# Gates' products at unit 4 in passes one and two, and one decay formed ahead of their Silu

## The chip, the cores and the metric

The kernel runs on one core of a Trainium2 chip. Its time is the device time of one execution in microseconds (us), and lower is better. The engines that matter here are PE (TensorE, matmuls), DVE (VectorE), ACT (ScalarE), POOL (GpSimd) and SP (the queue that issues the DMAs). Each works through its own instructions in order and waits for the others at semaphores.

## The reference, cut to what matters

Thirty-two images of 257 tokens with 256 features go through a small tower: a tokenizer, a layer of four state-space (Mamba) blocks with a mixture of experts, and a layer of attention with a routed feed-forward part. The change lies in the state-space blocks alone:

```python
def _mamba_block(x, in_w, conv_w, conv_b, A_log, xd_w, xB_w, xC_w, dtp_w, dtp_b, D, out_w, g, b):
    res = x
    xn = _layer_norm(x, g, b)
    xz = xn @ in_w
    xs, z = jnp.split(xz, 2, axis=-1)
    xc = conv(xs)                              # depthwise, 4 taps
    xc = silu(xc + conv_b)
    delta = softplus(xc @ xd_w @ dtp_w + dtp_b)
    Bm = xc @ xB_w
    Cm = xc @ xC_w
    A = -jnp.exp(A_log)
    dA = jnp.exp(delta[..., None] * A)         # the decays
    dBx = (delta * xc)[..., None] * Bm[:, :, None, :]
    y = _ssm_scan(dA, dBx, Cm) + D * xc        # h = dA_t * h + dBx_t ; y = sum_n h * C_t
    return y * jax.nn.silu(z) @ out_w + res    # silu(z): the gates
```

A block has 512 channels with 16 states each; two blocks run forward over the tokens and two backward.

## The kernel before

The program has two phases, the state-space blocks (`mamba_phase`) and the rest (`tail_phase`). The first takes the images in 16 groups of two. Each group has four jobs, one for each block. The first group's job 0 is written out ahead; a loop over 15 groups then holds jobs 1, 2, 3 and 4, where job 4 is job 0 of the next group; jobs 1, 2 and 3 of the last group follow. There are 64 jobs in all. "Pass one" and "pass two" are jobs 1 and 2.

A job is a scan over 64 states, 16 for each of four chunks of 128 channels. It is written as 32 units `u` of two states, `2u` and `2u+1`. For each state `s`:
- ACT forms the decay (L781), an Exp of 512 columns, into one of two banks (`decay`, by `s % 2`). It may do so once the scan of state `s-2` is through. ACT's unit `u` forms the decays `2u+2` and `2u+3`.
- POOL multiplies B by the input (`bu`, L543, four buffers).
- DVE scans (L982; L986 in the first chunk) and multiplies the result by C (L1002). For every fourth state POOL does this product (L555). The scans of a unit come first, its products behind them.
- PE adds the result to `y_ps` by transposes (L1239), in unit `u` the states `2u-2` and `2u-1`. With the first state of a chunk it multiplies the skip connection in front (L1232), which has to wait until ACT has copied the last chunk's rows out of `y_ps` to `y_t` (`token_rows`, L756; at units 1, 9, 17 and 25).

Everything else is placed by hand beside these units. The places the change touches are these:
- The gates of the job are four products `z0` to `z3` of PE (L1123, w_ps<-xn,in_w), one for each of the units from `gates_at(jj)`. ACT copies each to `sz` one unit later (L740). When all are there it takes the Silu of all of `sz` (L746). A table load stands in front of it, and one behind it (L747) brings the table for Exp and Ln back.
- The next job's norm begins at unit 9: PE forms the centred input in two products, `cen0` at unit 9 and `cen1` at unit 10 (L1123, w_ps<-x_f,mean_w and tok_mean, or x_b). ACT squares and copies each (L645, L648): the first behind decay 23, the second between decays 24 and 25.
- At unit 2 PE starts the last job's output projection, `o0` and `o1`, which ACT copies at units 4 and 5 (L767). DVE multiplies a chunk's rows by the gates (L1022), the first one in unit 13.

All products other than `y_ps` share three banks, `w_ps`. A table of names gives each product a slot; even slots use banks 0 and 1, odd ones 2 and 1, so each shares the middle bank with its neighbour. A bank is free when the readers of the earlier slot have counted up `work_read` for their parity. A name with one bank uses bank 0 or 2 alone.

```python
            def gates_at(jj):
                return 7 if jj == 4 else 5
            def silu_at(jj):
                return gates_at(jj) + 4, CONV_AT + 9
```

Of the kernel before, what the change touches and what calls it, by code (L numbers as in the profile page):

```python
# [5 lines left out]
ALU = mybir.AluOpType  # L6
# [19 lines left out]
DVE_C = STATES - len(POOL_C)  # L26
BLOCK_OF_JOB = (0, 2, 1, 3)
CONV_AT = 14
EPS = 1e-5
LOG_EXP = "natural_log_exp_and_others"  # L30
LN_SLACK = 2.0 ** -23
# [4 lines left out]
def mamba_phase(nc, a, h_mid, bc_dram, diag_dram, skip_dram):  # L36
# [18 lines left out]
    def one_job(jj, more):  # L55

        keys = [("y3", jj - 1)]
        keys += [("o0", jj - 1), ("o1", jj - 1)]
        keys += [("tmean", 4)] if jj == 3 and more else []
        keys += [("m0", 3), ("m1", 3)] if jj == 4 else []  # L60
        gates = [(name, jj) for name in gates_of_job]
        if jj == 3 and more:
            gates = gates[:1] + [("tvar", 4)] + gates[1:]
        return keys + gates + later_keys(jj, preparation(jj + 1, jj == 2 and more) if more or jj < 3 else [])
# [18 lines left out]

    def bank_count(name):

        return 1 if name in ("first", "y0", "y1", "y2", "y3") else NB

    slots = {key: i for i, key in enumerate(first_keys + body_keys)}
    final_slots = {key: n_first + i for i, key in enumerate(final_keys)}
# [6 lines left out]


    def gates_at(jj):
        return 7 if jj == 4 else 5

    def y_at(jj):
        return (14 if jj == 4 else 12), 18, 26
# [1 line left out]
    def silu_at(jj):  # L104

        return gates_at(jj) + 4, CONV_AT + 9

# [8 lines left out]
    def job_count(g, jj, per_job, k):  # L116

        return g * (4 * per_job) + (jj * per_job + k)
# [13 lines left out]
    def positive(count):  # L132

        return not isinstance(count, int) or count > 0
# [15 lines left out]
    with ExitStack() as ctx:  # L150
# [464 lines left out]
        def _(act):  # L615
# [150 lines left out]
                dst = o_f if jj % 4 == 2 else stream(jj)  # L766
                func(dst[:, c, :, :], w[:, :, 0:S], ACT.Identity).then_inc(read_of(name, g, jj), 1)  # L767

            def decays(g, jj, s):

                jj, s = on(jj, s)
                c, n = s // NST, s % NST
                k = BLOCK_OF_JOB[jj % 4]
                if n == 0 and c == 0:
                    act.wait_ge(delta_ready, job_count(g, jj, CI, c + 1))
                elif n == 0:
                    act.wait_ge(delta_reset, job_count(g, jj, CI - 1, c))

                if positive(job_count(g, jj, STATES, s + 1 - NDP)):
                    act.wait_ge(scan_done, job_count(g, jj, STATES, s + 1 - NDP))  # L780
                func(decay[:, s % NDP, :].rearrange("p (b t) -> p b t", b=NB), delta[:, c, :, 1:S], ACT.Exp,  # L781
                     scale=neg_a[:, k, c, n:n + 1]).then_inc(decays_ready, 1)

# [91 lines left out]
            def after_odd(g, jj, u, first, last):  # L875

                if u == 0:
                    softplus_powers(g, jj, 3)
                if u == 1:
                    softplus_log(g, jj, 3)  # L880
                if jj == 3 and not last and u == 5:
                    square_tokens(g, 4)
                if jj == 0 and u == 6 or jj == 4 and u == 8:
                    start_backward(g, jj + 1)
                if jj == 4 and u == 22:
                    copy_h(g, 4)
                if u == silu_at(jj)[0]:
                    gate_silu(g, jj)
                if last:
                    return  # L890
                if u == norm_at(jj) + 1:
                    centred(g, jj + 1, 0)
                if jj != 4 and u == norm_at(jj) + 4:
                    gain_and_bias(g, jj + 1)
                if u == CONV_AT + 1:
                    conv_input(g, jj + 1, 1)
                if u == silu_at(jj)[1]:
                    conv_silu(g, jj + 1)
                if u == CONV_AT + 11:
                    projections(g, jj + 1)  # L900
                if u in (CONV_AT + 12, CONV_AT + 13):
                    softplus_start(g, jj + 1, u - CONV_AT - 12)
                if u == CONV_AT + 14:
                    softplus_log(g, jj + 1, 0)
                if u == 31:
                    softplus_powers(g, jj + 1, 2)

            def lead(g, jj, s, last):

                if not (last and s >= STATES):  # L910
                    decays(g, jj, s)

            def period(g, jj, first, last):
                for u in range(UNITS):
# [15 lines left out]
        def _(dve):  # L930
# [34 lines left out]
            def h_slot(s):  # L965
                return len([v for v in range(s) if v not in POOL_C]) % NU

            def scan(g, jj, s, b):
                inside = s not in POOL_C
                if b == 0:  # L970
# [8 lines left out]
                h = h_ps[:, h_slot(s), :] if inside else ch[:, s % NPR, :]  # L979
                if s >= NST:  # L980

                    dve.tensor_tensor_scan(h, decay[:, s % NDP, :], bu[:, s % NBU, 0:NB * L], 0.0, ALU.mult, ALU.add  # L982
                                           ).then_inc(scan_done, 1)
                    return
                cols = slice(b * L, (b + 1) * L)
# [64 lines left out]
            def period(g, jj, first, last):  # L1050
                for u in range(UNITS):
# [15 lines left out]
                    if size:  # L1067
                        step_size(*size, 0)
                    scan(g, jj, s + 1, 0)
                    if s + 1 in POOL_C and s < NST:  # L1070
                        c_times_h(g, jj, s)
                        scan(g, jj, s + 1, 1)
                    else:
                        if s < NST:
                            scan(g, jj, s + 1, 1)
                        c_times_h(g, jj, s)
                        if s + 1 not in POOL_C:
                            c_times_h(g, jj, s + 1)
# [949 lines left out]
```

## Time and profile before

| | us |
|---|---|
| median of 3 runs | 10204.22 (10203.43 to 10209.12) |
| the profiled execution | 10211.62 |
| its span, first to last instruction | 10209.9 |
| mean granted clock of PE, as a share of the full one | 0.886 |

Over the span DVE is busy 79%, PE 81%, POOL 69% and ACT 58%. These shares mix two phases: in the state-space phase DVE and POOL are busiest, in the rest PE. The state-space phase ends near 8500 us. The clock stands in the profile as the share granted: 1.0 is 2.4 GHz and 0.5 is 1.2 GHz.

One logical matmul in float32 is two instructions in the trace, so a gate's product is a row of eight, and so is a pair of states. A timeline row gives its start, the time it covers, and in brackets how long the engine was idle before it and what ended that.

### The profile page before, as it was taken

Reading aid. Unit: us, or ns where it says so; the run is one execution under the profiler, and the core shown is the slowest. Engines: PE = TensorE matmul, PEld = TensorE weight load, DVE = VectorE, ACT = ScalarE, POOL = GpSimd, SP = SyncE. Lnnn points to the kernel's source line nnn. Section 1 sums busy time; section 2 is a strip of 40 time slices with the busy share of each in tenths; the row PEclk is TensorE's granted clock in tenths of the full one; section 3 lists DMA queues with packets and bytes.
Section 4 is the critical chain, followed back from the end, with each engine's and each line's share of the span. In section 5 each row is a group of like instructions: output and inputs, shape, how many; then the busy total and the mean of one; then the engine's idle time right before and its main releaser. Section 6 shows DMA issues by size and latency. Waiting matters only on the chain. (4 is left out here: it accounts for less than half of the span.)

```text
span 10209.9 us, 153036 instructions
## 1 busy us (share of the span) xinstructions
PE 8288.9 (81%) x42776; PEld 6783.2 (66%) x42776; DVE 8054.5 (79%) x10482; ACT 5907.1 (58%) x9202; POOL 7026.4 (69%) x7227
## 2 busy tenths in 40 slices
PE   5787878787878787878787878787878776999998
PEld 4666666666666666666666666666666664777776
DVE  4989898989898989898989898989898993333332
ACT  4656566666665666666666666666666662544443
POOL 4878788888888888888888888888888882000000
PEclk8888888888988888889898888888988887999998
DMA  2222222222222222222222222222222220000000
GB/s 92 99 90 94 100 94 98 95 99 94 97 97 91 94 96 96 98 96 94 89 89 86 94 94 100 94 99 93 100 94 100 94 84 24 11 12 8 12 10 9
DMA packets 414834, 818.78 MB, mean 80 GB/s; under 512 B 148918, under 2 KB 194138, under 8 KB 414042
## 3 DMA queue, kind: packets, MB, share of 16 engines
q1 hardware_dynamic: 410328, 806.69, 23.3%
q8 instruction: 331, 5.42, 0.2%
q14 instruction: 461, 3.78, 0.1%
q10 hardware_dynamic: 3714, 2.89, 0.1%
HBM read 783.16 MB, written 26.30 MB: 79 GB/s over the span
## 5 line engine op out<-in xcount | busy, mean ns | idle before, releaser
L781 ACT ACTIVATE decay<-delta,neg_a 128x512 f32<-128x512 f32 x4096 | 2799.4, 689 | 2378.0 <-DVE h_ps L982 1145.6
L543 POOL TENSOR_TENSOR bu<-b_all,u_buf 128x512 f32<-128x512 f32 x3072 | 3573.3, 1189 | 188.8 <-DVE h_ps L982 186.2
L982 DVE TENSOR_TENSOR_SCAN h_ps<-decay,bu 128x512 f32<-128x512 f32 x2304 | 2778.6, 1222 | 513.3 <-ACT decay L781 431.7
L1239 PE MATMUL y_ps<-ident,ch 128*128 128x128 f32 x16384 | 2504.0, 302 | 535.6 <-DVE ch L1002 412.8
L1239 PEld LDWEIGHTS y_ps<-ident,ch 128*128 128x128 f32 x16384 | 2132.8, 156 | 904.7 <-DVE ch L1002 552.4
L555 POOL TENSOR_TENSOR ch<-ch,c_all 128x512 f32<-128x512 f32 x1024 | 1326.3, 1295 | 966.9 <-DVE ch L982 779.1
L1002 DVE TENSOR_TENSOR ch<-h_ps,c_all 128x512 f32<-128x512 f32 x3072 | 1976.9, 671 | 0.0
L546 POOL TENSOR_TENSOR bu<-b_all,u_buf 128x514 f32<-128x514 f32 x1024 | 1244.8, 1236 | 12.7 <-DVE h_ps L982 9.1
L1123 PE MATMUL w_ps<-xn,in_w 128*128 128x257 f32 x4096 | 1095.1, 412 | 167.9 <-ACT xn L670 67.5
L986 DVE TENSOR_TENSOR_SCAN h_ps<-decay,bu 128x256 f32<-128x256 f32 x1536 | 1047.1, 737 | 59.2 <-POOL bu L546 33.9
L1123 PEld LDWEIGHTS w_ps<-xn,in_w 128*128 128x128 f32 x4096 | 806.9, 208 | 335.3 <-issue 75.7
L1582 POOL TENSOR_TENSOR rstd_F<-h_F 128x514 f32<-128x514 f32 x16 | 17.5, 1095 | 1425.6 <-DMA h_F<-h_mid 1425.6
L1123 PE MATMUL w_ps<-xs_pad,diag_store 128*128 128x257 f32 x4096 | 967.7, 381 | 10.5 <-ACT xc L697 10.5
L982 DVE TENSOR_TENSOR_SCAN ch<-decay,bu 128x512 f32<-128x512 f32 x768 | 923.5, 1202 | 23.7 <-ACT decay L781 22.3
L1123 PEld LDWEIGHTS w_ps<-xs_pad,diag_store 128*128 128x128 f32 x4096 | 741.7, 190 | 123.5 <-ACT xc L697 35.9
L1123 PE MATMUL w_ps<-sz,out_w 128*128 128x257 f32 x2048 | 498.9, 386 | 116.4 <-ACT x_b L767 52.4
L1123 PEld LDWEIGHTS w_ps<-sz,out_w 128*128 128x128 f32 x2048 | 375.4, 191 | 178.9 <-ACT x_b L767 59.7
L1123 PE MATMUL w_ps<-dtbc,dt_w 32*128 32x257 f32 x1024 | 397.5, 509 | 111.0 <-ACT rstd L723 107.4
L1232 PE MATMUL y_ps<-skip_diag,xc 128*128 128x128 f32 x2048 | 347.8, 324 | 150.1 <-ACT y_t L756 150.1
L1232 PEld LDWEIGHTS y_ps<-skip_diag,xc 128*128 128x128 f32 x2048 | 311.5, 230 | 213.7 <-ACT y_t L756 203.2
L1251 PE MATMUL w_ps<-ident,y_t 128*128 128x128 f32 x1024 | 187.0, 314 | 300.8 <-ACT y_t L756 300.8
L1123 PE MATMUL w_ps<-xc,xp_w 128*64 128x257 f32 x1024 | 270.9, 424 | 137.6 <-ACT xc L703 137.6
(262 smaller groups left out, 11512.5 us busy)
## 6 DMA issues: line engine op xcount, KB each, us to landing
b_all<-bc_dram SPq DMA_DIRECT2D x512, 514.0 KB, 6.4
c_all<-bc_dram SPq DMA_DIRECT2D x512, 514.0 KB, 7.4
in_w<-in_L_attn_in_w SPq DMA_DIRECT2D x64, 1024.0 KB, 5.0
diag_store<-diag_dram SPq DMA_DIRECT2D x256, 256.0 KB, 3.7
x_in<-in_x SPq DMA_DIRECT2D x128, 256.0 KB, 3.6
out_w<-in_L_attn_out_w SPq DMA_DIRECT2D x64, 512.0 KB, 3.9
skip_diag<-skip_dram SPq DMA_DIRECT2D x64, 256.0 KB, 4.4
h_mid<-h_cur SPq DMA_DIRECT2D x32, 257.0 KB, 2.2
```

The source lines that it names most:

```text
L543: pool.tensor_tensor(bu[:, s % NBU, 0:NB * L].rearrange("p (b t) -> p b t", b=NB), b_all[:, n // NU, n % NU, :, 1:], u_buf[:, c % 2, :, 1: ...
L546: pool.tensor_tensor(bu[:, s % NBU, :], b_all[:, n // NU, n % NU, :, :].rearrange("p b s -> p (b s)"), u_buf[:, c % 2, :, :].rearrange("p ...
L555: pool.tensor_tensor(h, h, c_all[:, n // NU, n % NU, :, 1:], ALU.mult).then_inc(pool_c_done, 1)
L781: func(decay[:, s % NDP, :].rearrange("p (b t) -> p b t", b=NB), delta[:, c, :, 1:S], ACT.Exp, scale=neg_a[:, k, c, n:n + 1]).then_inc(dec ...
L982: dve.tensor_tensor_scan(h, decay[:, s % NDP, :], bu[:, s % NBU, 0:NB * L], 0.0, ALU.mult, ALU.add).then_inc(scan_done, 1)
L986: last = dve.tensor_tensor_scan(h[:, cols], decay[:, s % NDP, cols], bu[:, s % NBU, b * S + 1:(b + 1) * S], bu[:, s % NBU, b * S:b * S + 1 ...
L1002: dve.tensor_tensor(ch[:, s % NPR, :].rearrange("p (b t) -> p b t", b=NB), h_ps[:, h_slot(s), :].rearrange("p (b t) -> p b t", b=NB), c_al ...
L1123: last = pe.matmul(w[0:rows, b, 0:S], lhs, rhs, start=(i == 0), stop=(i == len(terms(b)) - 1))
L1232: pe.matmul(y_ps[:, k, :], xc[:, jj % 2, c, b, 1 + half * P:1 + (half + 1) * P], skip_diag[:, jj % 2, c, :], start=(k == 0), stop=False, s ...
L1239: last = pe.matmul(y_ps[:, k, :], ch[:, s % NPR, k * P:(k + 1) * P], ident[:, :], is_transpose=True, start=False, stop=(n == NST - 1 and k ...
L1251: last = pe.matmul(w[:, k * P:(k + 1) * P], y_t[:, k, :], ident[:, :], is_transpose=True, start=True, stop=True, skip_group_check=True)
L1582: pool.tensor_tensor(rstd[s][:, :, :], h[s][:, 0, :, :], h[s][:, 1, :, :], ALU.add).then_inc(h_summed[s], 1)
```

## The change

- In every job but 3 and 4, `gates_at` is 4 instead of 5. Job 4 keeps 7 and job 3 keeps 5. The Silu, four units later, comes at unit 8 instead of 9 in jobs 1 and 2 (and in job 0 of the first group).
- In jobs 1 and 2 a new name, `early`, with one bank, follows `z3` in the table. In front of the Silu ACT forms decay 20 into that bank (`early_decay`), and leaves it out at its usual place. Decay 22, whose slot decay 20 no longer uses, waits for scan 18 alone.
- DVE takes decay 20 from that bank. Behind the issue of scan 21 it waits for scan 20 and counts the bank as read (`early_read`). PE's `cen1`, two slots on, waits for that count.

```diff
+EARLY = 20
@@
-        gates = [(name, jj) for name in gates_of_job]
+        gates = [(name, jj) for name in gates_of_job + (["early"] if jj in (1, 2) else [])]
@@
-        return 1 if name in ("first", "y0", "y1", "y2", "y3") else NB
+        return 1 if name in ("first", "early", "y0", "y1", "y2", "y3") else NB
@@
     def gates_at(jj):
-        return 7 if jj == 4 else 5
+        return {3: 5, 4: 7}.get(jj, 4)
@@
+            def early_decay(g, jj):
+
+                k = BLOCK_OF_JOB[jj % 4]
+                c, n = EARLY // NST, EARLY % NST
+                act.wait_ge(read_of("z2", g, jj), nth("z2", g, jj))
+                func(banks("early", g, jj).rearrange("p (b t) -> p b t", b=NB), delta[:, c, :, 1:S], ACT.Exp,
+                     scale=neg_a[:, k, c, n:n + 1]).then_inc(decays_ready, 1)
+                act.sem_inc(full_of("early", g, jj), 1)
+
-            def decays(g, jj, s):
+            def decays(g, jj, s, behind=0):
@@
-                if positive(job_count(g, jj, STATES, s + 1 - NDP)):
-                    act.wait_ge(scan_done, job_count(g, jj, STATES, s + 1 - NDP))
+                if positive(job_count(g, jj, STATES, s + 1 - NDP - behind)):
+                    act.wait_ge(scan_done, job_count(g, jj, STATES, s + 1 - NDP - behind))
@@
                 if u == silu_at(jj)[0]:
+                    if jj in (1, 2):
+                        early_decay(g, jj)
                     gate_silu(g, jj)
@@
             def lead(g, jj, s, last):
 
+                if jj in (1, 2) and s == EARLY:
+                    return
                 if not (last and s >= STATES):
-                    decays(g, jj, s)
+
+                    decays(g, jj, s, behind=NDP if jj in (1, 2) and s - NDP == EARLY else 0)
@@
+            def decay_of(g, jj, s):
+
+                return banks("early", g, jj) if jj in (1, 2) and s == EARLY else decay[:, s % NDP, :]
+
+            def early_read(g, jj):
+
+                dve.wait_ge(scan_done, job_count(g, jj, STATES, EARLY + 1))
+                dve.sem_inc(read_of("early", g, jj), 1)
+
@@
-                    dve.tensor_tensor_scan(h, decay[:, s % NDP, :], bu[:, s % NBU, 0:NB * L], 0.0, ALU.mult, ALU.add
+                    dve.tensor_tensor_scan(h, decay_of(g, jj, s), bu[:, s % NBU, 0:NB * L], 0.0, ALU.mult, ALU.add
@@
                     scan(g, jj, s + 1, 0)
+                    if s == EARLY and jj in (1, 2):
+                        early_read(g, jj)
```

**ACT around the gates' Silu, in job 1 of the loop.** `decay` rows are the decays, `sz` the gates, `y_t` the copy of the finished rows. Before, from the copy of the rows behind decay 20 to decay 23:

```order
L756 ACTIVATE y_t<-y_ps 128x512
L738 REGISTER_ALU
L740 ACTIVATE sz<-w_ps 128x514
L780 REGISTER_ALU
L781 ACTIVATE decay<-delta,neg_a 128x512
L746 ACT_TABLE_LOAD
L746 ACTIVATE sz<-sz 128x2056
L747 ACT_TABLE_LOAD
L780 REGISTER_ALU
L781 ACTIVATE decay<-delta,neg_a 128x512
L780 REGISTER_ALU
L781 ACTIVATE decay<-delta,neg_a 128x512
```

After, from decay 19 to decay 23 (L791 are the decays now, L775 the early one):

```order
L791 ACTIVATE decay<-delta,neg_a 128x512
L775 ACTIVATE w_ps<-delta,neg_a 128x512
L747 ACT_TABLE_LOAD
L747 ACTIVATE sz<-sz 128x2056
L748 ACT_TABLE_LOAD
L757 ACTIVATE y_t<-y_ps 128x512
L790 REGISTER_ALU
L791 ACTIVATE decay<-delta,neg_a 128x512
L790 REGISTER_ALU
L791 ACTIVATE decay<-delta,neg_a 128x512
L790 REGISTER_ALU
L791 ACTIVATE decay<-delta,neg_a 128x512
```

The copy of the rows stood ahead of the last gate, decay 21 and the Silu, and now stands behind the Silu; decays 21, 22 and 23 follow it, where 22 and 23 did.

**PE in the same stretch.** `y_ps<-ident,ch` are the states, four rows for each, `y_ps<-skip_diag,xc` the skip products. Before, from states 14 and 15 to the start of centre product 0:

```order
L1237 REGISTER_ALU
L1239 MATMUL y_ps<-ident,ch 128x128 x4
L1237 REGISTER_ALU
L1239 MATMUL y_ps<-ident,ch 128x128 x4
L1123 MATMUL w_ps<-xn,in_w 128x257 x4
L1227 REGISTER_ALU
L1232 MATMUL y_ps<-skip_diag,xc 128x128 x4
L1237 REGISTER_ALU
L1239 MATMUL y_ps<-ident,ch 128x128 x4
L1235 REGISTER_ALU
L1239 MATMUL y_ps<-ident,ch 128x128 x4
L1123 MATMUL w_ps<-x_f,tok_mean 128x257
```

After, from gate product 3 to the register set for centre product 0:

```order
L1149 MATMUL w_ps<-xn,in_w 128x257 x4
L1263 REGISTER_ALU
L1265 MATMUL y_ps<-ident,ch 128x128 x4
L1263 REGISTER_ALU
L1265 MATMUL y_ps<-ident,ch 128x128 x4
L1253 REGISTER_ALU
L1258 MATMUL y_ps<-skip_diag,xc 128x128 x4
L1263 REGISTER_ALU
L1265 MATMUL y_ps<-ident,ch 128x128 x4
L1261 REGISTER_ALU
L1265 MATMUL y_ps<-ident,ch 128x128 x4
L1135 REGISTER_ALU
```

The last gate's product stood between states 15 and the skip products, and now stands ahead of states 14 and 15.

## Rows read from the trace of the kernel before

**Rows 1.** Window sums of the first phase: busy us of each engine (instructions), clock, DMA.

```profile
147.00:8500.00 8353.00, 6663.27 (x35292) 5525.09 (x35293) 7524.75 (x9300) 5144.30 (x7971) 6979.05 (x7165) 0.87 0.28 94
```

(The engines of such a row are PE, PEld, DVE, ACT and POOL; behind them stand the granted clock, the share and the GB/s of the DMAs.)

**Rows 2.** Waits: who waited for whom, us in total, times, longest.

```profile
DVE h_ps L982 <- ACT decay L781: 431.7, 225, 8.6
```

**Rows 3.** Timeline of DVE: start, us, line, names, count, idle before.

```profile
2928.66 1.23 DVE L982 TENSOR_TENSOR_SCAN h_ps<-decay,bu 128x512 f32<-128x512 f32 x1
2929.80 1.20 DVE L982 TENSOR_TENSOR_SCAN ch<-decay,bu 128x512 f32<-128x512 f32 x1
...
2933.20 2.35 DVE L982 TENSOR_TENSOR_SCAN h_ps<-decay,bu 128x512 f32<-128x512 f32 x2 [1.62 <-ACT decay L781]
...
2936.64 1.22 DVE L982 TENSOR_TENSOR_SCAN h_ps<-decay,bu 128x512 f32<-128x512 f32 x1
2938.28 1.22 DVE L982 TENSOR_TENSOR_SCAN ch<-decay,bu 128x512 f32<-128x512 f32 x1 [0.42 <-ACT decay L781]
...
2941.61 0.69 DVE L1022 TENSOR_TENSOR sz<-w_ps,sz 128x512 f32<-128x512 f32 x1 [0.38 <-PE w_ps L1251]
2942.54 1.29 DVE L948 TENSOR_TENSOR cen<-cen,w_ps 128x514 f32<-128x514 f32 x2 [0.24 <-DVE sz L1022]
```

**Rows 4.** Timeline of ACT in the same stretch.

```profile
2923.85 0.69 ACT L781 ACTIVATE decay<-delta,neg_a 128x512 f32<-128x512 f32 x1
...
2926.20 0.58 ACT L756 ACTIVATE y_t<-y_ps 128x512 f32<-128x512 f32 x1
...
2927.86 1.28 ACT L746 ACT_TABLE_LOAD   x1
...
2932.39 1.30 ACT L781 ACTIVATE decay<-delta,neg_a 128x512 f32<-128x512 f32 x2
2933.63 0.58 ACT L645 ACTIVATE sq<-w_ps 128x514 f32<-128x514 f32 x1
...
2934.59 0.69 ACT L781 ACTIVATE decay<-delta,neg_a 128x512 f32<-128x512 f32 x1
```

**Rows 5.** Timeline of DVE: scan 22 in the first and the last of 32 jobs.

```profile
317.38 1.23 DVE L982 TENSOR_TENSOR_SCAN h_ps<-decay,bu 128x512 f32<-128x512 f32 x1 [1.62 <-ACT decay L781]
...
8294.23 1.23 DVE L982 TENSOR_TENSOR_SCAN h_ps<-decay,bu 128x512 f32<-128x512 f32 x1 [1.68 <-ACT decay L781]
```

**Rows 6.** Timeline of PE in the stretch of rows 3 and 4.

```profile
2922.51 1.04 PE L1239 MATMUL y_ps<-ident,ch 128*128 128x128 f32 x8
2923.38 1.90 PE L1123 MATMUL w_ps<-xn,in_w 128*128 128x257 f32 x8
2926.83 1.16 PE L1232 MATMUL y_ps<-skip_diag,xc 128*128 128x128 f32 x8 [1.55 <-ACT y_t L756]
...
2928.70 0.60 PE L1123 MATMUL w_ps<-x_f,tok_mean 128*128 128x257 f32 x2
...
2930.44 1.03 PE L1239 MATMUL y_ps<-ident,ch 128*128 128x128 f32 x8
...
2936.33 1.92 PE L1239 MATMUL y_ps<-ident,ch 128*128 128x128 f32 x8
```

**Rows 7.** Restarts of PE after idle time: timeline, then window sums.

```profile
278.41 0.90 PE L1251 MATMUL w_ps<-ident,y_t 128*128 128x128 f32 x3 [5.02 <-ACT y_t L756]
...
4335.23 3.25 PE L1239 MATMUL y_ps<-ident,ch 128*128 128x128 f32 x16
...
8379.49 0.47 PE L1251 MATMUL w_ps<-ident,y_t 128*128 128x128 f32 x1 [4.95 <-ACT y_t L756]
...
278.40:281.00 2.60, 2.59 (x12) 2.60 (x13) 1.84 (x4) 1.54 (x3) 2.60 (x4) 0.50 0.03 6
...
8379.50:8382.10 2.60, 2.60 (x12) 2.60 (x13) 1.98 (x4) 1.59 (x3) 2.60 (x4) 0.50 0.00 0
...
2945.61:2949.61 4.00, 4.00 (x15) 3.49 (x16) 4.00 (x5) 2.92 (x5) 3.29 (x7) 0.61 0.02 4
4332.61:4339.01 6.40, 6.40 (x32) 6.32 (x33) 5.74 (x10) 2.53 (x5) 3.87 (x5) 0.58 0.00 0
```

**Rows 8.** Timeline of ACT and DVE near unit 5 of the same job.

```profile
2912.12 0.58 ACT L767 ACTIVATE x_f<-w_ps 128x514 f32<-128x514 f32 x1
...
2915.66 0.73 DVE L986 TENSOR_TENSOR_SCAN ch<-decay,bu 128x256 f32<-128x256 f32 x1
```

## The prediction, made before the changed kernel was run

> **What bounds the kernel now.** I read the window sums by stage first. The state-space phase takes 8353 of 10210 us, and in it DVE is busy 7525 us, more than any other engine [rows 1]. So a microsecond counts there when DVE stands idle. The waits, read next, say for whom it is idle: its scans waited 431.7 us for decays from ACT [rows 2], its largest item in this phase. ACT is busy only 5144 us of the phase; it is short of time in places, and the Silu of the gates is one of them.
>
> The timelines of such a place follow, from a job of pass one. I name scans and decays by their state. The reader should go by the starts: a queued DVE instruction starts some 0.09 us before its forerunner's end (scan 21 at 2929.80, scan 20 until 2929.89). DVE starts scan 20 at 2928.66, scan 21 at 2929.80, and then waits 1.62 us for decay 22 [rows 3]. ACT explains it: it loads a table (2927.86), runs the Silu, loads the first table back, and starts decay 22 only at 2932.39 [rows 4]. The same wait stands in all 32 jobs of passes one and two, from the first to the last [rows 5]; 32 x 1.62 = 52 us is what this wait by itself can give back. A further 0.42 us before scan 25 and 0.38 us before the output product [rows 3] hang on PE's products.
>
> **What the change does there.** With the gates' products one unit earlier, the last gate is copied ahead of decay 19, which keeps its 2923.85; then come the early decay 20 and the Silu. A second decay starts 0.61 us after the first (two take 1.30, one 0.69 [rows 4]). From 2923.85 on:
> - Decay 20 runs 2924.46 to 2925.15. From the first table load to the first instruction behind the block it takes 2932.39 - 2927.86 = 4.53 us [rows 4], so with the load at 2925.17 the block ends at 2929.70.
> - y_t, the copy of the finished rows for PE, was at 2926.20. It now stands behind the block: 2929.70 to 2930.28.
> - Decay 21 starts 0.48 us after it starts (half of the 0.96 us of two such copies [rows 4]): 2930.20 to 2930.89. Decay 22 follows until 2931.50, since its slot needs scan 18 only.
>
> DVE starts scan 20 at 2928.66 as before. Scan 21 starts 0.12 us behind its decay (as 2933.20 stands behind 2932.39 + 0.69), at 2931.01 instead of 2929.80: 1.21 us of the stall has moved one scan forward. Scan 22 comes 33.20 - 29.80 - 1.62 - 0.09 = 1.69 us later when it needn't wait: 2932.70 instead of 2933.20. **Up to here the job gains 0.50 us**, not 1.62.
>
> **What the later y_t does.** PE's order is: states 14 and 15, the skip products (which wait for y_t), states 16 and 17, centre product 0, states 18 and 19, centre product 1. Before, PE had the last gate's product (2923.38) to do before its wait of 1.55 us [rows 6]. Now that product stands ahead of states 14 and 15. PE starts those at 2922.51 as before, has issued them by 2923.38, and idles until 2930.33, 6.9 us.
>
> What such a gap does to PE is in the trace. Between 147 and 8400 us PE restarts 137 times after more than 3.2 us of idle time. Each restart met the granted clock at 0.50 (1.2 GHz) or fell to it within 2 us; the first and the last stand in [rows 7]. The 4 us from the restart at 2945.61 have a mean clock of 0.61, so 2 x 0.39 x 4.00 = 3.1 us at half speed; the 6.4 us from the one at 4332.61 have 0.58, so 5.4 us [rows 7]. More than nine in ten lie below 5.6. At half speed eight instructions of a pair of states take 1.92 us (2936.33), at full 1.04: a factor of 1.85 [rows 6]. At full speed the skips and states 16 and 17 take 2928.70 - 2926.83 = 1.87 us, centre product 0 takes 1.74 (until 2930.44) and a pair of states 0.87 [rows 6].
>
> So skips and states run at half speed from 2930.33 to 2933.79, and then comes centre product 0. With a rise 4.25 us after the restart, midway between 3.1 and 5.4, it does 0.79 us at half speed (a quarter of 3.22) and the rest in 1.31: issued 2935.89, full 2936.09 with 0.2 us for the last matmul. ACT, which has decay 23 done by 2933.03, waits for it. Then:
> - The two copies of centre 0 take 0.96 us [rows 4] to the start of decay 24: 2937.10 to 2937.79. Scan 24 starts at 2937.91 instead of 2936.64.
> - PE, at full speed again, does states 18 and 19 and the two halves of centre product 1, 0.87 us each: full 2938.70. Its copies start at 2938.75, decay 25 at 2939.71, done 2940.40; scan 25 starts at 2940.52 instead of 2938.28.
> - The output product comes 41.61 - 38.28 - 0.38 - 0.09 = 2.86 us behind scan 25 when it needn't wait [rows 3]: 2943.38 instead of 2941.61. PE has its rows by 2942.7, so it adds no wait.
>
> **From there on everything is 1.77 us later**, and nothing behind takes it back: the norm, the convolution and the next job's loads follow DVE's own progress. With 3.1 us at half speed the same working gives +1.41 us a job, with 5.4 us +2.30.
>
> **The other edits.** The first job has its gates at unit 4 too, without the early decay; its decay 20 then stands behind the block as well, and I give it the same 1.77 us. Gate product 0 stands at unit 4, where its second half waits for ACT's copy of o1 (2912.12 + 0.58 = 2912.70) [rows 8]. It is full near 2913.8, ACT asks for it right away, and decay 13 is done near 2915.0. Scan 13 starts at 2915.66 [rows 8]: free, with 0.5 us of cover; if the cover went, each microsecond beyond it would cost 32 us in all. PE's new wait for the early bank ends once scan 20 is through, before centre product 1: free. The new semaphore instruction on DVE, between scan 21 and the product of state 20, is shown by no row. The nearest is the 0.24 us of idle time behind the output product [rows 3], where such an instruction stands. I take 0 of 0 to 0.24 us, since the product behind waits for the same scan anyway (at most 8 us in all). SP may load the next weights 2.6 us earlier, for which nobody waits.
>
> **The sum.** 33 x 1.77 = 58 us. The profiled execution took 10211.6 us (span 10209.9), the median of the runs is 10204.2; those 7 us are no part of the change, so I add to the median: **10262 us**. This case's own range is +47 to +76 us, 10251 to 10280.
>
> **A rule against the trace.** Transposes make up much of PE's work after such a restart. Behind 4332.61 it had 4 transposes of rows, 8 skip instructions and 16 of states, and the clock rose 5.4 us later, within or right behind those sixteen, which took 3.25 us where two eights at half speed take 3.8 [rows 7]. The Trainium skill, TensorE: Matmul & The Clock Gate, Part 4: PE-mode transpose, states that transposes don't count as busy in the same way and that the full clock doesn't engage for them. By that rule the sum would be that of the first rival; this trace speaks against it.
>
> **Rivals.**
> - *The clock stays low longer* (slower still). If it rose only after centre product 1, centre 0 would be full at 2937.21, states 18 and 19 would take 1.61 us and the two halves 3.22: full at 2942.04, scan 25 at 2943.86, +5.1 us a job, 10372 us. For it: little but transposes runs after the gap. Against it: most restarts rose sooner. 5%.
> - *PE keeps pace* (same). At 2.4 GHz centre product 0 is full at 2934.14 and decay 24 done by 2935.84, in time for scan 24 (2936.14). Centre product 1 is full at 2936.74, decay 25 done at 2938.44; scan 25 starts at 2938.56 and the output product at 2941.42: -0.19 us a job, 10198 us. The clock alone decides it. Against it: no such restart kept the full clock. Slack behind the output product that I don't see, and that absorbs most of 1.77 us, ends here too. 15%.
> - *The stall goes altogether* (faster). DVE doesn't starve at scans 21 to 25, and 1.62 + 0.42 = 2.04 us go in each of 32 jobs: -65 us, 10139 us. For it: this is where DVE waits, and an early decay is one scan (1.14 us) of cover. It takes over if decay 21 is there by 2929.7 and centre 0 by 2935.0. Against it: by the rows the block alone ends at 2929.70, and decay 21 stands behind block and y_t. 13%.
>
> **Chances.** Forecast 67%, longer low clock 5%, same 15%, faster 13%. A measurement of this kernel can tell about 0.2% (20 us) from no change: faster 0.13, same 0.15, slower 0.72. The range of 10190 to 10300 us takes in the forecast with both bounds, 20 us of misjudged pitches above, and the even case below; it leaves out the full gain and the longer low clock.
>
> **What would show it.** In the profile after: 1.2 us of waiting at scan 21 and none at scan 22 (first step); a gap of PE near 6.9 us before the skip products of these jobs, and a granted clock of 0.50 behind it (second); ACT waiting 3 us for centre product 0, and DVE 1.7 us at scan 24 and 1.5 at scan 25 (third); from scan 20 to the output product 14.7 us instead of 12.95. The forecast is wrong if the skips run at full speed, if y_t isn't behind the block, or if jobs grow by another amount than that distance.

## The result, and the profile after

| | before | after |
|---|---|---|
| median, us | 10206.67 (4 runs) | 10303.64 (4 runs) |
| ratio, with its 95% interval | | 1.0097 (1.0085 to 1.0109) |
| profiled execution, us | 10211.62 | 10303.99 |
| its span, us | 10209.9 | 10302.3 |

The change costs 97 us, 0.97%. The forecast was 58 us slower with a range up to 10300: the sign and the chain of causes were right, the size was too small by 39 us, and the time lies 4 us above the range.

The waits of the whole run answer to [rows 2]. DVE waits 458.1 us for decays at the scans into `h_ps` instead of 431.7, and 91.5 instead of 22.3 at those into `ch`, 95.6 us more in all. PE's wait of the skip products for y_t has doubled. Before, then after:

```profile
PE y_ps L1232 <- ACT y_t L756: 150.1, 99, 3.8
DVE ch L982 <- ACT decay L781: 22.3, 48, 0.6
```

```profile
DVE h_ps L1006 <- ACT decay L791: 458.1, 220, 7.7
DVE ch L1006 <- ACT decay L791: 91.5, 103, 1.3
PE y_ps L1258 <- ACT y_t L757: 308.1, 82, 6.8
```

The same job that the prediction worked through follows, first the timeline of ACT (against [rows 4]):

```profile
2951.43 0.69 ACT L791 ACTIVATE decay<-delta,neg_a 128x512 f32<-128x512 f32 x1
2952.06 0.67 ACT L775 ACTIVATE w_ps<-delta,neg_a 128x512 f32<-128x512 f32 x1
2952.75 1.28 ACT L747 ACT_TABLE_LOAD   x1
2954.05 1.92 ACT L747 ACTIVATE sz<-sz 128x2056 f32<-128x2056 f32 x1
2955.98 1.28 ACT L748 ACT_TABLE_LOAD   x1
2957.27 0.60 ACT L757 ACTIVATE y_t<-y_ps 128x512 f32<-128x512 f32 x1
2957.77 1.29 ACT L791 ACTIVATE decay<-delta,neg_a 128x512 f32<-128x512 f32 x2
2959.75 0.69 ACT L791 ACTIVATE decay<-delta,neg_a 128x512 f32<-128x512 f32 x1 [0.69 <-DVE ch L1006]
2964.02 0.60 ACT L646 ACTIVATE sq<-w_ps 128x514 f32<-128x514 f32 x1 [3.58 <-PE w_ps L1149]
```

Then PE (against [rows 6]) and the granted clock of the 6 us from its restart, 0.60, so 2 x 0.40 x 6.00 = 4.8 us at half speed. (The eight rows of a pair of states are one instruction for each of its eight transposes, not two as for the other float32 products.)

```profile
2950.09 1.03 PE L1265 MATMUL y_ps<-ident,ch 128*128 128x128 f32 x8
2957.92 2.07 PE L1258 MATMUL y_ps<-skip_diag,xc 128*128 128x128 f32 x8 [6.80 <-ACT y_t L757]
2959.79 1.91 PE L1265 MATMUL y_ps<-ident,ch 128*128 128x128 f32 x8
2961.50 1.07 PE L1149 MATMUL w_ps<-x_f,tok_mean 128*128 128x257 f32 x2
...
2963.82 1.03 PE L1265 MATMUL y_ps<-ident,ch 128*128 128x128 f32 x8
...
2957.92:2963.92 6.00, 6.00 (x25) 5.58 (x26) 5.23 (x6) 1.83 (x3) 4.35 (x5) 0.60 0.00 0
```

And DVE (against [rows 3]), scans 20, 21, 22 and 23, 24, 25, and the output product:

```profile
2956.24 1.23 DVE L1006 TENSOR_TENSOR_SCAN h_ps<-w_ps,bu 128x512 f32<-128x512 f32 x1
2958.49 1.23 DVE L1006 TENSOR_TENSOR_SCAN ch<-decay,bu 128x512 f32<-128x512 f32 x1 [1.02 <-ACT decay L791]
...
2960.21 2.34 DVE L1006 TENSOR_TENSOR_SCAN h_ps<-decay,bu 128x512 f32<-128x512 f32 x2
...
2966.17 1.23 DVE L1006 TENSOR_TENSOR_SCAN h_ps<-decay,bu 128x512 f32<-128x512 f32 x1 [2.45 <-ACT decay L791]
2968.33 1.22 DVE L1006 TENSOR_TENSOR_SCAN ch<-decay,bu 128x512 f32<-128x512 f32 x1 [0.93 <-ACT decay L791]
...
2971.18 0.67 DVE L1046 TENSOR_TENSOR sz<-w_ps,sz 128x512 f32<-128x512 f32 x1
```

The reader should see the order of events: the Silu block, y_t behind it, PE idle for 6.80 us, eight skip instructions in 2.07 us instead of 1.16, ACT waiting 3.58 us for centre product 0, and DVE waiting for decay 24, which stands behind the copies of that product. From scan 20 to the output product it is now 14.94 us instead of 12.95.

Averaged over the jobs, from the starts of the scans (us, jobs 1 and 2 of 16 groups, one trace each):

| stretch | job 1 before | after | job 2 before | after |
|---|---|---|---|---|
| scan 20 to 22 | 4.55 | 3.98 | 4.55 | 3.98 |
| 22 to 24 | 3.44 | 5.75 | 3.44 | 5.88 |
| 24 to 25 | 1.44 | 2.18 | 1.29 | 2.52 |
| 25 to 27 | 5.44 | 4.98 | 5.42 | 4.96 |
| 27 to 48 | 37.62 | 38.02 | 37.47 | 37.50 |
| 48 to 63 | 29.51 | 29.57 | 36.84 | 37.76 |

From the unrounded averages the loss up to scan 27 is 2.02 us in job 1 and 2.66 in job 2, behind it 0.45 and 0.95. For 16 jobs of each kind that is 75 and 23 us. The first job adds 2.4, the rest of the difference of 92 us between the spans is a few us less elsewhere, most of it in job 3.

### The profile page after: what moved, and what is told of

The parts are those of the page before. It is cut to its first block and busy times, and to the rows that moved or that the text cites. A ratio compares the mean times of both kernels' runs of the same rounds, so it can differ in the third digit from the quotient of the medians.

```text
span 10302.3 us, 152980 instructions
## 1 busy us (share of the span) xinstructions
PE 8338.6 (81%) x42776; PEld 6827.9 (66%) x42776; DVE 8060.5 (78%) x10482; ACT 5911.6 (57%) x9202; POOL 7023.7 (68%) x7227
## 3 DMA queue, kind: packets, MB, share of 16 engines
q8 instruction: 332, 5.44, 0.2%
## 5 line engine op out<-in xcount | busy, mean ns | idle before, releaser
L791 ACT ACTIVATE decay<-delta,neg_a 128x512 f32<-128x512 f32 x4064 | 2776.7, 689 | 2301.4 <-DVE h_ps L1006 1101.2
L1006 DVE TENSOR_TENSOR_SCAN h_ps<-decay,bu 128x512 f32<-128x512 f32 x2272 | 2737.8, 1221 | 547.9 <-ACT decay L791 458.1
L1006 DVE TENSOR_TENSOR_SCAN ch<-decay,bu 128x512 f32<-128x512 f32 x768 | 924.4, 1204 | 92.7 <-ACT decay L791 91.5
L1258 PE MATMUL y_ps<-skip_diag,xc 128*128 128x128 f32 x2048 | 375.7, 342 | 308.1 <-ACT y_t L757 308.1
L1258 PEld LDWEIGHTS y_ps<-skip_diag,xc 128*128 128x128 f32 x2048 | 337.7, 247 | 362.4 <-ACT y_t L757 345.9
L1149 PE MATMUL w_ps<-xc,xp_w 128*64 128x257 f32 x1024 | 295.6, 453 | 137.7 <-ACT xc L704 137.7
```

What stands on the lines that cost most here:

```text
L1006: dve.tensor_tensor_scan(h, decay_of(g, jj, s), bu[:, s % NBU, 0:NB * L], 0.0, ALU.mult, ALU.add).then_inc(scan_done, 1)
L1149: last = pe.matmul(w[0:rows, b, 0:S], lhs, rhs, start=(i == 0), stop=(i == len(terms(b)) - 1))
L1258: pe.matmul(y_ps[:, k, :], xc[:, jj % 2, c, b, 1 + half * P:1 + (half + 1) * P], skip_diag[:, jj % 2, c, :], start=(k == 0), stop=False, s ...
```

## The experiments

Each kernel was timed beside the kernel before on the same chip, and the ratios are to those runs. Since the kernel before had other medians there (10200.0 us beside the first four experiments, 10203.1 and 10203.6 beside the others), the ratios are the fairer comparison. The expectations name three theories. By A the late rows starve PE, and the half clock delays centre product 0. By B the early decay and its bank cost the time. By C the gates' products at unit 4 cost it.

| experiment | median, us | ratio (95% interval) |
|---|---|---|
| rows ahead of the Silu | 10208.8 | 1.0008 (0.9998 to 1.0018) |
| no early decay | 10310.2 | 1.0107 (1.0090 to 1.0124) |
| gates at unit 4 alone | 10196.4 | 0.9994 (0.9984 to 1.0004) |
| before, rows behind the Silu | 10365.6 | 1.0164 (1.0147 to 1.0181) |
| PE's gap filled | 10226.3 | 1.0024 (1.0014 to 1.0034) |
| centre product 0 first | 10221.5 | 1.0018 (1.0008 to 1.0028) |
| decay 22 early | 10223.9 | 1.0018 (1.0008 to 1.0027) |
| decay 22 early, gates at unit 4 | 10189.1 | 0.9985 (0.9975 to 0.9995) |
| the same, centre product 0 first | 10219.2 | 1.0014 (1.0004 to 1.0024) |

### The rows' copy alone, in both directions

From the changed kernel, the copy of the rows is moved ahead of the early decay:

```diff
                     if jj in (1, 2):
+                        token_rows(g, jj, 0)
                         early_decay(g, jj)
@@
-                    if u % PAIRS == 1 and not (first and u == 1):
+                    if u % PAIRS == 1 and not (first and u == 1) and not (jj in (1, 2) and u == 9):
                         token_rows(g, jj - (u == 1), (u // PAIRS - 1) % CI)
```

> The changed kernel, but in jobs 1 and 2 ACT copies the finished rows (y_t) ahead of the early decay and the Silu instead of behind them. Theory A (the late copy of the rows starves PE, PE restarts at half clock, and centre product 0 comes too late for decay 24) expects the gap of PE before the skip products to fall from 6.8 us to under 1.5, the waits at scans 24 and 25 to vanish or nearly so, and 10180 to 10200 us. Theory B (the early decay itself, its bank and PE's wait for it) expects no change from the changed kernel, 10300 us. Theory C (the gates' products at unit 4 delay the start of the job) expects the same 10300 us.

And from the kernel before, the only change is that in jobs 1 and 2 this copy goes behind the Silu:

```diff
                 if u == silu_at(jj)[0]:
                     gate_silu(g, jj)
+                    if jj in (1, 2):
+                        token_rows(g, jj, 0)
@@
-                    if u % PAIRS == 1 and not (first and u == 1):
+                    if u % PAIRS == 1 and not (first and u == 1) and not (jj in (1, 2) and u == 9):
                         token_rows(g, jj - (u == 1), (u // PAIRS - 1) % CI)
```

> The kernel before, gates at unit 5 and Silu at unit 9, with one thing changed: in jobs 1 and 2 ACT copies the rows behind the Silu instead of two decays ahead of it. Theory A expects the loss without any part of the change: the copy 6.2 us later, a gap of PE near 7.5 us, half clock for 4 to 6 us behind it, scan 24 some 4 us later and 4 to 5 us a job in all, 10330 to 10370 us. Theories B and C expect it within 20 us of the kernel before, since neither the bank nor the gates move.

The first took 10208.8 us, 0.08% more than the kernel before with an interval that takes in no change: it gives back some nine tenths of the loss, with the early decay, its bank and the early gates all in place. The second took 10365.6 us, 1.64% more than the kernel before and in the range expected, with none of them. That decides for A against B and C as the cause of the loss. The first came out 9 us above the range expected, though. Its timeline of DVE in a job 2 shows what becomes there of the 0.5 us gained at scan 22:

```profile
3058.23 1.22 DVE L1007 TENSOR_TENSOR_SCAN ch<-decay,bu 128x512 f32<-128x512 f32 x1 [1.01 <-ACT decay L791]
...
3065.05 1.22 DVE L1007 TENSOR_TENSOR_SCAN ch<-decay,bu 128x512 f32<-128x512 f32 x1 [0.45 <-ACT decay L791]
...
3069.31 0.69 DVE L1047 TENSOR_TENSOR sz<-w_ps,sz 128x512 f32<-128x512 f32 x1 [1.31 <-PE w_ps L1278]
```

The output product waits 1.31 us for PE. The stall moved on to the next product that PE owes DVE. This holds for job 2 alone: up to scan 27 the 16 jobs 2 take 15.04 us on average instead of 14.69, while the jobs 1 keep their gain with 14.14 instead of 14.87. And the early bank isn't free here. In all 32 jobs PE waits some 1.3 us in front of centre product 1 until DVE gives the bank back, a wait that the changed kernel doesn't have:

```profile
PE w_ps L1150 <- DVEq L991: 41.3, 32, 1.3
```

How much of the missing gain this wait costs isn't shown.

The second shows the mechanism at a larger size, in its PE and DVE timelines of a job 2:

```profile
3106.09 2.08 PE L1234 MATMUL y_ps<-skip_diag,xc 128*128 128x128 f32 x8 [7.29 <-ACT y_t L756]
...
3106.74 2.35 DVE L984 TENSOR_TENSOR_SCAN h_ps<-decay,bu 128x512 f32<-128x512 f32 x2 [1.65 <-ACT decay L781]
...
3113.45 1.23 DVE L984 TENSOR_TENSOR_SCAN h_ps<-decay,bu 128x512 f32<-128x512 f32 x1 [3.19 <-ACT decay L781]
```

The old wait at scan 22 is untouched (1.65), and a new one of 3.19 us stands at scan 24 (3.85 us in job 1 and 3.37 in job 2 on average).

### The other parts alone

Without the early decay (the kernel before, with only `gates_at` as in the change):

```diff
     def gates_at(jj):
-        return 7 if jj == 4 else 5
+        return {3: 5, 4: 7}.get(jj, 4)
```

> The kernel before with the gates' products at unit 4 and the Silu at unit 8 in all jobs but 3 and 4, without the early decay: decay 20 is formed at its usual place, behind the Silu. Theory A expects the copy of the rows to come one more decay later (0.6 us), so some 0.65 us a job more than the changed kernel: 10320 to 10330 us. Theory B (the early decay and its bank are the cost) expects it to be near the kernel before, 10205 us.

It took 10310.2 us, about 7 us more than the changed kernel's 10303.6, and its interval alone reaches 17 us to both sides. A expected 10320 to 10330, so this came out 10 us below its range. The early decay doesn't cause the loss, and whether it saves any of it can't be told from this; B's 10205 us is excluded.

With the gates' products at unit 4 and the Silu left at unit 9:

```diff
-        return gates_at(jj) + 4, CONV_AT + 9
+        return (11 if jj == 4 else 9), CONV_AT + 9
```

> The kernel before with the gates' products at unit 4 in all jobs but 3 and 4; the Silu stays at unit 9, behind the copy of the rows, and there is no early decay. Theory C (the products at unit 4 cost) expects a part of the 97 us, 10230 us or more. Theories A and B expect the last gate's copy out of the way of decay 21, so the Silu 0.4 us earlier and scan 22 with it: 0 to -0.4 us in 32 jobs, 10190 to 10205 us.

It took 10196.4 us, the median of ten executions of which one took 28395 us, and is within the noise of the kernel before. C is excluded: in sum the products at unit 4 cost nothing, as the prediction had it. The sum hides two parts, though. From scan 20 to 27 the jobs 1 and 2 take 14.00 us on average instead of 14.78, and from scan 27 to 63 they take 0.5 us more (0.43 in job 1 and 0.53 in job 2). The section on what repeats comes back to this.

### How much of it is the clock

The changed kernel, with centre product 0 formed three times into its own banks in front of the skip products:

```diff
+                    if jj in (1, 2) and u == 9 and not last:
+                        for _ in range(3):
+                            centre_ahead(g, jj + 1)
                     if not (first and u == 0):
                         add_state(g, jj, NU * u - 2)
```

> The changed kernel with PE's gap filled: in jobs 1 and 2, in front of the skip products that wait for the rows, PE forms centre product 0 three times into its own banks (24 instructions, 5.2 us at full speed); the real one still stands behind states 16 and 17. The copy of the rows stays late. This takes the half clock away and leaves the late copy. If the half clock is what costs, PE restarts at full speed, centre product 0 is full 2 us or more earlier, and the time is near that worked out for the rival at full clock, 10195 to 10215 us. If the late copy alone costs, most of the 97 us stay: 10270 us or more.

It took 10226.3 us, 1.0024 of the kernel before where the changed one has 1.0097. The rows come as late as in the changed kernel, 1.67 us behind the start of scan 20, and yet three quarters of the loss are gone. Its timelines of PE, ACT and DVE in a job 2:

```profile
3058.72 1.16 PE L1272 MATMUL y_ps<-skip_diag,xc 128*128 128x128 f32 x8 [0.82 <-ACT y_t L757]
...
3062.52 0.60 ACT L646 ACTIVATE sq<-w_ps 128x514 f32<-128x514 f32 x1 [1.29 <-PE w_ps L1149]
...
3064.43 1.22 DVE L1006 TENSOR_TENSOR_SCAN h_ps<-decay,bu 128x512 f32<-128x512 f32 x1
3066.84 1.22 DVE L1006 TENSOR_TENSOR_SCAN ch<-decay,bu 128x512 f32<-128x512 f32 x1 [1.18 <-ACT decay L791]
```

The skips run at full speed (1.16 us), ACT waits 1.29 us instead of 3.58, scan 24 waits for nothing. The granted clock is 1.00 from scan 20 to scan 25 in all 32 jobs. From scan 20 to scan 27 such a job takes 14.76 us on average, against 14.78 in the kernel before: the even rival of the prediction, with its 0.19 us less, was a fair account of what full clock gives up to there. The time missed the expected 10195 to 10215 by 11 us. What is left stands mostly behind scan 48 of job 2 (37.68 us, as the 37.76 of the changed kernel, against 36.84 before), not here.

Then centre product 0 ahead of the skip products, so that it needn't wait for the rows:

```diff
+                    if jj in (1, 2) and u == 9 and not last:
+                        centre(g, jj + 1, [0])
                     if not (first and u == 0):
                         add_state(g, jj, NU * u - 2)
@@
-                    if u in (norm_at(jj), norm_at(jj) + 1):
+                    if u in (norm_at(jj), norm_at(jj) + 1) and not (jj in (1, 2) and u == 9):
```

> The changed kernel with PE's order altered in jobs 1 and 2: centre product 0 stands ahead of the skip products and states 16 and 17, so it doesn't wait for the rows. The rows stay late and PE still has a gap of some 5 us before them. Theory A (centre product 0 late) expects ACT to find centre 0 at once, no wait at scan 24, a smaller one at scan 25 since states 16 to 19 and centre 1 still follow a gap: 10190 to 10230 us. If what counts is the gap and the half clock by themselves, whatever stands behind, 10280 us or more.

It took 10221.5 us, in the range expected. PE still idles 4.28 us and restarts at half speed (skips 2.08 us), but scan 24 finds its decay, and scan 25 waits 0.91 us (1.43 on average):

```profile
3058.16 2.08 PE L1258 MATMUL y_ps<-skip_diag,xc 128*128 128x128 f32 x8 [4.28 <-ACT y_t L757]
3060.03 2.50 PE L1265 MATMUL y_ps<-ident,ch 128*128 128x128 f32 x16
...
3063.88 1.22 DVE L1006 TENSOR_TENSOR_SCAN h_ps<-decay,bu 128x512 f32<-128x512 f32 x1
3066.01 1.22 DVE L1006 TENSOR_TENSOR_SCAN ch<-decay,bu 128x512 f32<-128x512 f32 x1 [0.91 <-ACT decay L791]
```

So the gap and the half clock cost most where a product that ACT needs stands close behind them. From scan 20 to 27 the jobs take 15.02 us here, 0.24 more than before the change.

### The early decay at the other side of the rows

The changed kernel with `EARLY = 22` and gates and Silu at their old units, and then with the gates' products at unit 4 and the Silu at unit 9. In both the rows are copied ahead of the Silu, as before.

> The early decay at the other side of the rows' copy: gates at unit 5 and Silu at unit 9 as before the change, copy of the rows ahead of the Silu as before, and in jobs 1 and 2 decay 22 formed into the idle bank in front of the Silu. Theory A expects no late rows: scan 22 without a wait, the stall of 1.62 us at scan 23 as 1.1 us, so 0.5 us a job less up to there, of which centre product 1 may take some back: 10188 to 10206 us. Theory B (the early bank costs) expects 10250 us or more.

> As the last one, with the gates' products at unit 4 in all jobs but 3 and 4 and the Silu still at unit 9: nothing of the gates stands between decay 20 and the Silu any more, so the block starts 0.4 to 0.5 us earlier than in the last one. Theory A expects 0 to 16 us less than that one: 10175 to 10200 us. Theory B expects 10250 us or more.

The first took 10223.9 us, slower than the kernel before by 0.18% and outside the 10188 to 10206 expected. The trace puts this miss down mostly to the early bank. From scan 20 to 24 the jobs gain 0.50 us as forecast. But the bank is given back behind scan 23 here, PE waits for it in front of centre product 1 in all 32 jobs (85.4 us in all, 2.8 at most), and scan 25, whose decay stands behind the copies of that product, waits 1.02 us in job 1 and 1.57 in job 2 on average, where it waited 0.25 and 0.10 before the change. The waits of the run, and a job 2:

```profile
PE w_ps L1149 <- DVEq L990: 85.4, 32, 2.8
```

```profile
3065.30 0.70 PE L1149 MATMUL w_ps<-x_b,mean_w 128*128 128x257 f32 x2 [2.84 <-DVEq L990]
...
3069.94 1.22 DVE L1006 TENSOR_TENSOR_SCAN ch<-decay,bu 128x512 f32<-128x512 f32 x1 [1.58 <-ACT decay L791]
```

So B's wait is real where PE is otherwise on time, though it has no part in the loss of the changed kernel, where no such wait stands.

The second took 10189.1 us, 0.15% faster, in the range expected, with the interval below 1 and a median below both kernels. PE waits only 13.1 us for the bank there. In its DVE timeline, of a job 2, scan 22 waits for nothing, scan 23 0.64 us, and scan 25 takes 1.05 us back:

```profile
3047.05 1.22 DVE L1006 TENSOR_TENSOR_SCAN h_ps<-w_ps,bu 128x512 f32<-128x512 f32 x1
3048.91 1.23 DVE L1006 TENSOR_TENSOR_SCAN h_ps<-decay,bu 128x512 f32<-128x512 f32 x1 [0.64 <-ACT decay L791]
...
3053.51 1.22 DVE L1006 TENSOR_TENSOR_SCAN ch<-decay,bu 128x512 f32<-128x512 f32 x1 [1.05 <-ACT decay L791]
```

Then the second once more, with centre product 0 ahead of the skip products as above.

> The eighth experiment (gates at unit 4, Silu at 9, decay 22 early), with centre product 0 ahead of the skip products in jobs 1 and 2. It halves PE's gap of 3.3 us before the rows. If half clock behind this gap still costs there (unit 12 of job 2 was 0.9 us longer than before), 5 to 25 us less than the eighth: 10165 to 10185 us. If centre product 1, which waits for the early bank, is what binds, no change from it: 10185 to 10195 us.

It took 10219.2 us, 30 us more, where no change or less was expected. PE, in a job 2:

```profile
3063.16 1.23 PE L1149 MATMUL w_ps<-x_b,mean_w 128*128 128x257 f32 x2 [4.10 <-DVEq L990]
...
3063.16:3068.20 5.04, 5.04 (x16) 4.20 (x17) 3.05 (x4) 2.18 (x5) 3.07 (x3) 0.52 0.00 2
```

With product 0 done early, PE has nothing left before product 1, which waits 4.10 us for DVE to give the early bank back (L990). The gap is now in front of product 1, the granted clock behind it 0.52, and scan 25 waits 2.48 us. The change of order closed one hole and opened another that costs more. Most of it falls on job 2, which takes 1.84 us more up to scan 27, where job 1 takes 0.48.

### What repeats from one execution to the next

The two kernels were traced a second time.

> The kernel before, unchanged, for a second trace. The prediction took the length of the half clock and the baseline from one trace. If the clock's falls and rises lie at other places of a job from one execution to the next, jobs 1 and 2 show half clock in other units than in the first trace, units 12 and 27 differ by 0.2 to 0.5 us a job, and the sum of the state-space phase moves by up to 20 us. If they are tied to the instructions, every unit repeats within 0.05 us. Time 10190 to 10213 us either way.

> The changed kernel, unchanged, for a second trace. If the rise of the clock after PE's 6.8 us gap isn't tied to the instructions, its delay (4.4 us on average in job 1, 5.5 in job 2 of the first trace) lies elsewhere between 3 and 6 us here, and centre 0 moves with it. If it is tied to them, the averages repeat within 0.1 us. Time 10295 to 10312 us either way.

The times were 10215.3 us, 2 us above the range expected, and 10297.2 us, inside it; each is a single execution. Of 6 us from the restarts of the same two jobs, the changed kernel's second trace has 0.61 (job 1) and 0.59 (job 2); the first had 0.60 and, in job 2, 0.50, which is 4.7, 4.9, 4.8 and 6.0 us at half speed. First the first trace's, then the second's:

```profile
3086.37:3092.37 6.00, 6.00 (x22) 5.54 (x23) 5.24 (x6) 1.83 (x3) 4.35 (x5) 0.50 0.00 1
```

```profile
3091.53:3097.53 6.00, 6.00 (x25) 5.54 (x25) 5.23 (x6) 1.83 (x3) 4.35 (x5) 0.59 0.02 6
2962.08:2968.08 6.00, 6.00 (x26) 5.60 (x27) 5.23 (x6) 1.83 (x3) 4.37 (x5) 0.61 0.01 2
```

In a single job the rise comes at another time in another execution. The averages repeat better than that, though not within the 0.1 us that the expectation set for a clock tied to the instructions: over 16 groups the half clock lasts 4.36 us in job 1 and 5.33 in job 2, then 4.67 and 5.20. In the kernel before, the stretch from scan 20 to 27 repeats within 0.13 us. So neither branch of the two expectations holds as it was put. The loss, taken between the second traces, is 2.26 and 2.73 us up to scan 27 (2.02 and 2.66 in the first), and 0.60 and 0.40 behind it (0.45 and 0.95). The stretch from 48 to 63 of job 2 grows by 0.49 us there instead of 0.92: part of the longer end repeats. The 8 us before scan 52 of a job 2 have the full clock in both traces of the kernel before (the first is shown), and 0.79 in both of the changed one (again the first):

```profile
3107.20:3115.30 8.10, 5.07 (x28) 3.24 (x28) 6.35 (x7) 7.28 (x9) 8.10 (x9) 1.00 0.00 0
```

```profile
3140.00:3148.10 8.10, 5.98 (x22) 3.28 (x21) 6.37 (x8) 6.94 (x9) 8.10 (x9) 0.79 0.01 2
```

Behind it the next output product waits 0.33 us for its rows and the scan after it 0.38 us more, where before only the 0.38 stood. From scan 54 to 56 job 2 takes 4.95 and 4.94 us after, 4.51 and 4.50 before. So these stretches of half clock are tied to the kernel, though no instruction near them was changed. They aren't tied to the early decay or the late rows either. With the gates moved alone the jobs 2 take 37.29 us from scan 48 to 63, with the rows' copy moved alone 37.58, where the kernel before has 36.84 and 36.89. With centre product 0 first in the changed kernel it is 36.88, with only decay 22 early 36.56.

## Why the prediction was too low

**What bounds, and the first gain: right.** DVE's starts gave the time. ACT's schedule came out as worked out: y_t 5.84 us behind decay 19 (forecast 5.85), decay 21 at 6.34 (6.35). Scans 20 to 22 gained 0.57 us a job, where 0.50 was forecast.

**The gap and the half clock behind it: right in kind.** The gap was 6.80 us (6.9), the restart at 0.50, and scan 24 and scan 25 waited, 2.45 and 0.93 us in this job where 1.7 and 1.5 were forecast. The experiments with the rows' copy in both directions show the cause, the one with the filled gap shows that the clock, not the delay of y_t as such, carries about three quarters of it, and nearly all of it up to scan 27. The sentence that nothing behind takes the loss back held.

**Three terms of the sum were mis-sized.** The forecast was 1.77 us for 33 jobs. Measured were 2.34 us up to scan 27 and 0.70 behind it, on average of jobs 1 and 2. The job that was worked through lost 1.99 us up to its output product (14.94 instead of 12.95), so for that job the forecast was near.
- *The length of the half clock.* I took 4.25 us, midway between two restarts. The 32 restarts of interest averaged 4.36 us in job 1 and 5.33 in job 2, 4.85 in all. The trace of before couldn't have given this figure: its 137 restarts average 4.12 us, which is near what I took, and only one of them follows a gap of more than 5.5 us. Why the half clock lasts longer behind this gap stays open. It is about 0.3 us a job, since centre product 0 at half speed loses nearly half of each further microsecond.
- *The baseline.* The job I worked through had waits of 0.42 us at scan 25 and ran 15.09 us from scan 20 to 27; the average of the 32 jobs was 14.78. Against an average job the same schedule costs 0.3 us more: after the change that job took 17.07 us, the average one 17.12. That is the step that starts from "instead of 2941.61".
- *"From there on everything is 1.77 us later".* Wrong by 0.7 us a job, 23 us. Job 1 lost 0.45 us behind scan 27 and job 2 0.95 (0.60 and 0.40 in the second traces). Some 0.4 us of it in each, which repeats (0.65 in job 1 of the second traces), stands where PE now runs at half clock before unit 16 of job 1 and unit 27 of job 2. What put the half clock there is not explained; that it follows from the moved length of the jobs is a guess.

One sum of the range was off as well: with 3.1 us at half speed the same working gives +1.24 us a job, not +1.41, so the range of the case began at +41 us instead of +47. The time missed the range on its other side, so nothing hangs on it.

**The other edits: right.** Gates at unit 4 alone: 0.9994 (0.9984 to 1.0004). The new wait on the early bank cost nothing in this kernel, since PE came to it late. It isn't free in itself: with the rows on time PE waited 41.3 us for the bank, with decay 22 early 85.4, and in the last experiment it became the gap itself.

**The rivals.** The long low clock (rise only after centre product 1) didn't happen in any of the 32 jobs, the longest half clock being 6.0 us. On the rule of the Trainium skill that the prediction cites (TensorE: Matmul & The Clock Gate, Part 4: PE-mode transpose), by which the full clock doesn't engage for transposes, these jobs alone say little, since in 28 of them the rise lies within centre product 0, whose instructions aren't transposes. The experiment with centre product 0 first says more: in 31 of its 32 jobs the rise lies within the sixteen transposes behind the skip products (in the job shown they take 2.50 us, where twice 1.91 would be half speed), so the full clock did come while they ran. The even rival described what the filled gap gives. The full gain didn't come near in any kernel. Its point of decision, decay 21 by 2929.7, was missed by the Silu block itself.

## What to carry to other kernels

When an instruction group is moved earlier on an engine, list what it is moved ahead of, not only what it waits for: here the Silu overtook one copy of 0.6 us on ACT, and PE had nothing else to do until that copy. On PE, price a new idle gap by what stands behind it in order and is needed by others; the half clock after the gap can cost more than the gap. Take a baseline that varies from job to job as the average over all places that the change touches, not from the one job that was drawn. Where the trace has no gap as long as the one forecast, let the range allow for a longer half clock than any average of it shows. And an early bank has to be given back: look up which product waits for it, since that wait binds as soon as the others are gone.

## What the runs showed that I had not expected

- The stretches of half clock are much the same in two executions of one kernel when averaged over the groups (4.36 and 4.67 us, 5.33 and 5.20), but a change at unit 8 gives some before unit 16 of job 1 and at unit 25 of job 2 where there were none, or less.
- Extra work can be worth it: 24 instructions of PE in each of 32 jobs, whose result is overwritten, brought the changed kernel from 1.0097 to 1.0024 of the kernel before, by keeping the granted clock at 1.00.
- An improvement in one product's place moved the gap to the next (10189.1 to 10219.2 us), so here the question was less whether PE has an idle stretch than which product stands behind it.
